# Local attention scored once in 32x32 blocks, a front stage in two bank pairs, and work moved between ScalarE, GpSimd and VectorE

## The reference

```
x = x + attn_a(layernorm(x))   # 16 heads of 8, RoPE, causal over all 256 rows
x = x + ffn(layernorm(x))
x = x + attn_b(layernorm(x))   # 16 heads of 8, causal in windows of 32 rows, q and k rms-normalised with ln_w
x = x + ffn(layernorm(x))
ffn(x): gate, y = q4(x) @ q4(w_gate).T, q4(x) @ q4(w_up).T;  q4(silu(gate) * y) @ q4(w_down).T
```

## Time and profile before

| | us |
|---|---|
| median of three runs | 544.67 |
| the runs | 544.23, 544.67, 548.21 |
| span of the profiled execution, first to last instruction | 543.8 |

### The profile page before, as it was taken

How to read it: one execution, slowest core, us unless ns; L and a number is a source line. 1 busy time by engine, 2 the same in 40 slices (tenths; PEclk the granted TensorE clock), 3 DMA queues, 4 the chain that set the end, 5 groups by cost and what they waited for, 6 DMA issues and landing times.

```text
span 543.8 us, 10363 instructions
## 1 busy us (share of the span) xinstructions
PE 396.0 (73%) x4061; PEld 254.1 (47%) x4061; DVE 356.7 (66%) x894; ACT 202.9 (37%) x548; POOL 176.3 (32%) x207
## 2 busy tenths in 40 slices
PE   0031777587686789979978989889996958769543
PEld 0021434455455446745755665565563544344312
DVE  2982704746754855977899988898779584542531
ACT  1001052171371067266347437536633613414100
POOL 9512031213333053153247333612542514210302
PEclk9999968888897889979989999998997997867755
DMA  7105050030163036026216313410400502400000
GB/s 226 36 0 118 1 120 2 23 97 2 31 149 59 3 99 138 3 61 143 36 34 149 70 31 93 107 21 7 117 13 17 111 2 65 64 14 0 5 6 10
DMA packets 59936, 31.03 MB, mean 57 GB/s; under 512 B 3248, under 2 KB 59504, under 8 KB 59888
## 3 DMA queue, kind: packets, MB, share of 16 engines
q1 hardware_dynamic: 59888, 30.37, 24.1%
HBM read 16.14 MB, written 13.63 MB: 55 GB/s over the span
## 4 chain that ended last, share of the span: by engine, by line
PE 52%; DVE 22%; ACT 8%; DMA 6%; POOL 5%; issue 3%; SPq 3%; POOLq 0%; ACTq 0%; DVEq 0%
PE bank L889 7%; DVE bmax L1252 6%; PE bank L726 4%; PE bank L904 4%; PE bank L850 4%; PE bank L858 4%; PE bank L845 3%; PE bank L694 3%; PE bank L765 3%; PE bank L780 3%; PE bank L897 2%; DMA Qf<-nmTf 2%; PE bank L705 2%; PE bank L807 2%; PE bank L748 2%
## 5 line engine op out<-in xcount | busy, mean ns | idle before, releaser
L1252 DVE TENSOR_REDUCE bmax<-bank 128x3 f32<-128x384 f32 x128 | 62.3, 550 | 13.8 <-PE bank L750 12.7
L963 ACT ACTIVATE prob<-bank 128x384 f32<-128x384 f32 x128 | 56.6, 494 | 23.0 <-PE bank L769 21.6
L1006 ACT ACTIVATE probl<-bank 128x512 f32<-128x512 f32 x64 | 38.2, 598 | 40.3 <-PE bank L850 39.6
L765 PE MATMUL bank<-Qf,Kf 128*128 128x256 bf16 x128 | 28.3, 308 | 24.0 <-DMA Qf<-nmTf 17.5
L1324 DVE SCALAR_TENSOR_TENSOR fb__hg<-fb__th,bank 128x352 f32<-128x352 f32 x16 | 8.3, 520 | 36.2 <-ACT fb__th L1024 35.9
L889 PE MATMUL bank<-wguT,fb__xqT 128*128 128x352 f32 x64 | 27.6, 561 | 3.2 <-DVE fb__h L1325 1.7
L780 PE MATMUL bank<-prob,Vf 128*32 128x128 f32 (+1 forms) x512 | 28.6, 342 | 1.8 <-ACT oTf L924 1.8
L845 PE MATMUL bank<-maskb,identb 128*128 128x512 bf16 x64 | 25.7, 401 | 5.6 <-ACT probl L1006 4.0
L924 ACT ACTIVATE xnTf<-bank 128x256 f32<-128x256 f32 x8 | 3.1, 384 | 71.5 <-PE bank L694 71.5
L1103 POOL TENSOR_TENSOR fb__w<-fb__w,fb__c 128x704 f32<-128x704 f32 x8 | 13.4, 1679 | 49.3 <-DVE fb__w L1214 49.3
L765 PEld LDWEIGHTS bank<-Qf,Kf 128*128 128x128 bf16 x128 | 9.2, 102 | 42.4 <-DMA Qf<-nmTf 19.4
(11 more groups left out here) (212 smaller groups left out, 996.2 us busy)
## 6 DMA issues: line engine op xcount, KB each, us to landing
scr_f<-partsf SPq DMA_DIRECT2D x16, 192.0 KB, 2.4
Qf<-scr_f SPq DMA_DIRECT2D x16, 192.0 KB
Kf<-scr_f SPq DMA_DIRECT2D x16, 192.0 KB
scr_l<-partsl SPq DMA_DIRECT2D x16, 192.0 KB, 3.3
Ql<-scr_l SPq DMA_DIRECT2D x16, 192.0 KB, 3.5
Kl<-scr_l SPq DMA_DIRECT2D x16, 192.0 KB, 4.8
scr_f<-partsf SPq DMA_DIRECT2D x16, 128.0 KB, 1.9
scr_l<-partsl SPq DMA_DIRECT2D x16, 128.0 KB, 2.6
```

The costliest lines, as they stand in the source:

```text
L765: pe.matmul(ring(2 * g + j)[:, 0:256], Kf[:, g, 0:128], Qf[:, 2 * g + j, 0:256], start=True, stop=True)
L963: act.activation(prob[:, h % 8, :], bank[h % 3][:, 0:384], ACT.Exp).then_inc(f.s_exp, 1)
L1006: act.activation(probl[:, u % 2, :, :].rearrange("p c n -> p (c n)"), bank[4][:, :], ACT.Exp).then_inc(l.s_exp, 1)
L1252: dve.tensor_reduce(bmax[:, h, :], bank[h % 4][:, 0:384].rearrange("p (n k) -> p n k", k=P), AX.X, ALU.max).then_inc(bmax_done, 1)
```

## The change

- The local stage keeps q, k and v in fp32 and on the chip: nothing goes through DRAM. The keys are spread into four masked copies (`Kd`, GpSimd), so that one matmul over 32 partitions scores a window of 32 rows against the keys of four heads: 32 matmuls of 32 rows by 32 by 128 columns over all four row quarters and four column quarters of the array, in two halves with a wait between them (l_half). VectorE takes all maxima in one instruction and PE subtracts them with two fp32 matmuls with the identity (512 columns each). ScalarE takes exp of 2 x 512 columns, with q's rms factor as its scale. VectorE transposes in 32x32 blocks (1024 columns), and 128 matmuls of 32x32 by 9 columns, one per window, head and tile, give the outputs already in row order.
- The front stage's first pass runs in banks 0 and 1 and its second pass (now stage front3) in banks 2 and 3. Stacks and v have three homes (RING). Heads use their own 48, 51 or 64 partitions of the array instead of all 128: no zero rows are kept, a head is scored by two matmuls of 256 and 128 columns and masked by two of 256 and 128. The first pass of a batch may run beside the second pass of the batch before it.
- In both FFNs and for the weights, ScalarE makes the rounding constant (`step_of`: Abs, then Exp) that VectorE made from exponent bits or, for the weights, by compares.
- GpSimd centres the layernorms (`norm`) in place of VectorE; ScalarE puts v in its home.
- Masks and the rows of ones come ready from DRAM; GpSimd no longer fills stacks at the start. Loads of later x are steps in SP's order.
- Dependent VectorE instructions are steps of their own. TIMES and FFN_TURNS are new: FFN b's first turn comes after the third of FFN a rather than the fourth.

```diff
+RING = 3
+
+SLOTS = [0, 1, 2, 3, 4, 5, "o0", 6, 7, 8, 9, "o1", 10, 11, 12, 13, "o2", 14, 15, "o3"]
+VL = HD + 1
...
-        zrows = sb("zrows", [3 * PAIRS, SEQ], BF16)
+        Qfs = [sb(f"Qf{i}", [P, PAIRS, SEQ], BF16) for i in range(RING)]
+        Kfs = [sb(f"Kf{i}", [P, PAIRS, SEQ], BF16) for i in range(RING)]
+        Vfs = [sb(f"Vf{i}", [P, T, H, VW]) for i in range(RING)]
...
+                if b >= RING:
+                    sp.wait_ge(f_st_ps, (b - RING + 1) * H)
+                sp.wait_ge(f_wrote, (b + 1) * 16 * 6)
+                for m, dst in enumerate((Qfs[b % RING], Kfs[b % RING])):
...
+                        sp.dma_start(dst[64 * r:64 * r + NSTACK, :, :], src).then_inc(f_stack[b % RING], 16)
...
-                    if g == 0:
-                        pe.wait_ge(f.s_stack[b % 2], (b // 2 + 1) * 96)
-                        pe.wait_ge(f.s_v, b + 1)
-                        pe.wait_ge(rope_mul, b + 1)
-                        if b > 0:
-                            pe.wait_ge(f.s_done, b)
-                    if g >= 2:
-                        pe.wait_ge(bmax_done, b * H + 2 * g - 2)
-                    for j in range(2):
-                        pe.matmul(ring4(2 * g + j)[:, 0:128], Qf[:, 2 * g + j, 0:128], Kf[:, g, 0:128], start=True, stop=True)
-                    for j in range(2):
-                        pe.matmul(ring4(2 * g + j)[:, 128:384], Qf[:, 2 * g + j, 128:256], Kf[:, g, 0:256], start=False, stop=True, skip_group_check=True)
-                    for j in range(2):
-                        pe.matmul(ends(ring4(2 * g + j)), identb[:, :], mask_qk, start=False, stop=True, skip_group_check=True).then_inc(f.s_sc_ps, 1)
+                    if h == 0:
+                        pe.wait_ge(f_stack[b % RING], (b // RING + 1) * 64)
+                        if b < NBATCH - 1:
+                            pe.wait_ge(rope_mul, 2 * (b + 2))
+                            pe.wait_ge(f.s_v, b + 2)
+                        else:
+                            pe.wait_ge(f_nmT, b)
+                        if b == 0:
+                            pe.wait_ge(k_loaded, 16 * (1 + 2 * RING))
+                    if h >= 2:
+                        pe.wait_ge(bmax_done, b * H + h - 1)
+                    g, r = h // 2, h % 2
+                    S = fb[:, r, :]
+                    k = slice(64 * r, 64 * r + NSTACK)
+                    half_ = slice(64 * r, 64 * r + 64)
+                    pe.matmul(S[:, 0:256], Qf[k, g, 128:256], Kf[k, g, 0:256], start=True, stop=True, skip_group_check=True)
+                    pe.matmul(S[:, 256:384], Qf[k, g, 0:128], Kf[k, g, 0:128], start=False, stop=True, skip_group_check=True)
+                    pe.matmul(two(S[:, 128:384], 0, 128), eye_lo[half_, :], twice(m_qk[half_, :]), start=False, stop=True, skip_group_check=True)
+                    mm = pe.matmul(two(S[:, 128:384], 64, 64), eye_hi[half_, :], twice(m_qk[half_, 0:64]), start=False, stop=True, skip_group_check=True)
+                    mm.then_inc(f.s_sc_ps, 1)
                 yield
...
+            def front3(b):
+                Qf, Kf = Qfs[b % RING], Kfs[b % RING]
+                for n, slot in enumerate(SLOTS):
                     yield
...
+                    if n >= 2:
+                        if SLOTS[n - 2] in range(H):
+                            pe.wait_ge(f.s_exp, b * H + SLOTS[n - 2] + 1)
+                        else:
+                            pe.wait_ge(f_oT, b * GROUPS + int(SLOTS[n - 2][1]) + 1)
+                    elif b > 0:
+                        pe.wait_ge((f.s_aT, f.s_done)[n], b)
+                    S = fb[:, 2 + n % 2, :]
+                    if slot in range(H):
+                        if slot == 0:
+                            pe.wait_ge(f_nm_loaded, (b + 1) * 32)
+                        g, r = slot // 2, slot % 2
+                        k = slice(64 * r, 64 * r + KROWS)
+                        half_ = slice(64 * r, 64 * r + 64)
+                        pe.matmul(S[:, 128:384], Kf[k, g, 0:128], Qf[k, g, 0:256], start=True, stop=True, skip_group_check=True)
+                        pe.matmul(S[:, 0:128], Kf[k, g, 128:256], Qf[k, g, 128:256], start=False, stop=True, skip_group_check=True)
+                        pe.matmul(two(S[:, 0:256], 0, 128), eye_hi[half_, :], twice(m_kq[half_, :]), start=False, stop=True, skip_group_check=True)
+                        mm = pe.matmul(two(S[:, 0:256], 0, 64), eye_lo[half_, :], twice(m_kq[half_, 64:128]), start=False, stop=True, skip_group_check=True)
+                        mm.then_inc(f_st_ps, 1)
...
                 if b > 0:
-                    pe.wait_ge(l.s_nmT, b)
-                    if b > 1:
-                        pe.wait_ge(l.s_done, b - 1)
-                turn(bank[5], flat(xnl)).then_inc(l.s_xnT_ps, 1)
+                    pe.wait_ge(l.s_done, b)
...
+                for i in range(2):
+                    pe.matmul(lb[:, i, :], identb, mask_loc.unsqueeze(1).to_broadcast([P, 2, T * P]), start=True, stop=True, skip_group_check=True)
+                for gg in range(2):
+                    c0 = gg * T * P
+                    if gg:
+                        mm.then_inc(l_half, 1)
+                        yield
+                        pe.wait_ge(l_half, b + 1)
+                    for t in range(T):
+                        for n in range(NWIN):
+                            k0 = t * P + n * LS
+                            for i in range(2):
+                                g = 2 * gg + i
+                                rows = slice(32 * g, 32 * g + 32)
+                                mm = pe.matmul(lb[n * LS:(n + 1) * LS, i, c0 + t * P:c0 + (t + 1) * P], qkTl[rows, 0, k0:k0 + LS],
+                                               Kd[rows, :, k0:k0 + LS], start=False, stop=True, skip_group_check=True)
                 mm.then_inc(l.s_sc_ps, 1)
...
-                for u in range(2 * GROUPS + 1):
...
-                            pe.wait_ge(l.s_exp, b * 2 * GROUPS + u)
-                        k = slice((u % 2) * P, (u % 2 + 1) * P)
-                        pe.matmul(bank[4][:, :], identb[:, :], mask_blk, start=True, stop=True)
-                        side = u // 4
-                        r = slice(64 * side, 64 * side + KROWS)
-                        for j in range(4):
-                            g = 4 * (u // 2 % 2) + j
-                            mm = pe.matmul(bank[4][:, j * P:(j + 1) * P], Kl[r, g, k], Ql[r, g, k], start=False, stop=True, skip_group_check=True)
-                        mm.then_inc(l.s_st_ps, 1)
...
+                for i in range(2):
+                    mm = pe.matmul(lb[:, i, :], identf, nmaxl[:, 16 * i:16 * i + 16].unsqueeze(2).to_broadcast([P, 16, LS]),
+                                   start=False, stop=True, skip_group_check=True)
+                mm.then_inc(l_mx_ps, 1)
+                yield
+                pe.wait_ge(l_probT, b + 1)
+                for t in range(T):
+                    for c in range(H):
+                        h = 4 * (2 * (c // 4 % 2) + c // 8) + c % 4
+                        for n in range(NWIN):
+                            rows = slice(n * LS, (n + 1) * LS)
+                            mm = pe.matmul(lb[rows, 0, (t * H + h) * VL:(t * H + h + 1) * VL], probT[rows, c // 4, t, c % 4 * LS:(c % 4 + 1) * LS],
+                                           Vl[rows, t, h, :], start=True, stop=True, skip_group_check=True)
+                mm.then_inc(l.s_o_ps, 1)
...
+            def step_of(dst, src, absd, done, n):
+
+                act.activation(dst, src, ACT.Abs).then_inc(absd, 1)
+                act.wait_ge(absd, n)
+                act.activation(dst, dst, ACT.Exp, scale=STEP * LN2, bias=lift[:, 0:1]).then_inc(done, 1)
...
+                act.wait_ge(l_mx_ps, b + 1)
+                s5 = lb[:, :, :].rearrange("p i (g t k) -> p (i g) t k", g=2, t=T)
+                for t in range(T):
+                    ins = act.activation(probl[:, :, t, :], s5[:, :, t, :], ACT.Exp, scale=rql[:, 1, t:t + 1])
...
+            def norm(b, a, src, mv, rs, dst):
...
+                pool.wait_ge(a.s_rstd, 2 * b + 2)
+                for t in range(T):
+                    ins = pool.tensor_scalar(dst[:, t, :], src[:, t, :], mv[:, t, 0:1], rs[:, 1, t:t + 1], ALU.subtract, ALU.mult)
+                ins.then_inc(a.s_xn, 1)
...
+                pool.wait_ge(l_qkT, b + 1)
+                pool.tensor_tensor(Kd[:, :, :], qkTl[:, 1, :].unsqueeze(1).to_broadcast([P, 4, SEQ]),
+                                   hm.unsqueeze(2).to_broadcast([P, 4, SEQ]), ALU.mult).then_inc(l_kd, 1)
...
-            def centre(b, a, src, mv, rs, dst):
-                dve.wait_ge(a.s_rstd, 2 * b + 2)
-                for t in range(T):
-                    ins = dve.tensor_scalar(dst[:, t, :], src[:, t, :], mv[:, t, 0:1], rs[:, 1, t:t + 1], ALU.subtract, ALU.mult)
...
-                link(dve.tensor_scalar(c[:, :].bitcast(I32), u[:, :].bitcast(I32), 0x7F800000, None, ALU.bitwise_and))
```

(54 more changed lines are left out.)

1252 lines of the change are left out of this document (573 added, 679 removed), and 89 rows, old and new, of tables (FFN_TURNS, TIMES).

## The result

The changed kernel takes 474.6 us (median of 4 runs, 473.34 to 482.57) against 545.75 us for the one before beside it: a ratio of 0.868, 95% interval 0.863 to 0.873. The profiled execution has a span of 472.1 us and took 473.86. Executions of one kernel fall into faster ones and some that take about 2% longer at a lower granted clock; medians here are of all of them, ratios of the fast ones alone. The forecast was 462, with a range of 438 to 515.

A forecast was written before the change was run, and what follows sets the result against it. Neither PE nor DVE was taken as full over the whole; waits mattered, with PE 90% and DVE 84% busy in the steady part. Fill 66 + middle 293 + drain 101 = 460 us, plus a little: 462, range 438 to 515.

The forecast's parts named there:

- Fill: Start to the first front's sum: 66 us for 89.9, first scores at 30, first front done 36 us later.
- PE's work per batch: PE over all stages: local -2.6, front heads +0.9, tiling changes +1.1, net -0.6 us a batch, 348 to 343.
- My bounds for the heads: Front's heads on PE, 768 columns a pass for 640: 0 to 1.8 us more a batch, 0.9 taken.
- DVE's relief: VectorE per batch: about 7.5 us less work, busy 73% for 84%.
- The middle: Seven fronts after the first: 258 us of PE work at a rate of 0.88, 293 us.
- Rival 1: Middle: the chain across engines keeps PE's rate at 0.78, 331 us, total 499; chance 0.15.
- The period I said would be near 41: Middle: expected sign that fronts would follow each other at periods near 41 us, for 44.9 before.
- Drain: After the last front: FFN a, local, FFN b of batch 7 one behind the other, 67 + 32 + 2 = 101 us for 148.
- Rival 2: Middle: FFN banks take turns as before, the period stays 44.9, 314 us, total 482; chance 0.15.
- the sign that I had set: Middle: the prediction counts as wrong if, among other signs, the period of the fronts stays at 45.
- Rival 3: Local stage's output matmuls cost 45 ns each, +7.5 us a batch, total 530; chance 0.06.
- Rival 4: Output matmuls: four row quarters writing one bank wait for each other; slower overall from about 52 ns a record; chance 0.05.

The follow-up runs named there:

- Run 7: Kernel after, with VectorE first clearing a tile 24 times, each with a wait, before its first step: 505.34 us, ratio 0.925.
- runs 3 and 4: Kernel after, output matmuls issued twice (533.64 us), and separately the same 256 issued row quarter by row quarter (524.91 us, ratio 0.963).
- run 10: Kernel after, FFN a's last down phase moved ahead of FFN b's up phase of batch 5, engines' steps reordered to match: 504.33 us, ratio 0.918.
- run 12: Kernel after, with all layernorm centrings and both FFNs' rounding constants put back on VectorE together: 514.08 us, ratio 0.939.
- run 1: Kernel after, with all four centrings of a batch back on VectorE, GpSimd keeping only the root: 490.64 us, ratio 0.902.
- run 4: Kernel after, same 256 output matmuls with the window outermost, 64 in a row in one row quarter and column quarter: 524.91 us, ratio 0.963.

## Why the prediction came out right, and where its steps did not

The forecast was 12 us low in the span, and the three terms are off by +5.8, -10.6 and +16.9. That it came so near is partly luck: the middle's term hides two larger errors against each other, and it in turn makes up for most of the drain's.

**Fill, 66 for 71.8.** First projection at 9.5 as forecast; first scores at 31.9 for 30. The chain of 20.8 us through DRAM became 22.4, with a wait for V at its end. The first front then took 39.9 us for the 36 that I carried over: I gave the first pass of batch 1 beside it 16 x 0.28 us of PE, which went into PE's work but not into the fill's 66; that it is the 3.9 us was not tried. Run 7 shows that what the fill takes counts in full.

**PE's work per batch, -0.6 forecast, about -5.3 measured** (42/8), the term that was mis-sized most. With local taken out of both kernels, local lost 35 us or 4.4 a batch where I had -2.6, although the output matmuls hold PE for 5.6 us where I had 4.0 (records at the 9.5 ns of the earlier trace rows, measured 9.6, and on top waits for issue, 18.0 us in all). The front with the FFNs lost 0.8 a batch where I had +2.0. My bounds for the heads, 0 to 1.8 us more, allowed an overlap only at the last mask of a head. A pair side by side overlaps whole: 0.45 us where the 0.44 ns a column of the earlier trace rows gives 0.68, and less than the 0.56 of before, with the change to the next matmul in it, for which I had added 0.09 us apart. 55 of 128 pairs stand so. That this is what makes -0.8 of +2.0 fits, and no run tried it alone.

**DVE's relief, -7.5 a batch.** The page gives 356.7 - 271.6 = 85 us. Constants, casts and weights at the start take some 33 us of it before and 7 after, which leaves 59, or 7.3 a batch; the size was right. DVE is 185.87/282.4 = 66% busy in the middle, 73% forecast.

**The middle, 293 for 282, by two errors that cancel.** Work 218 for 258, rate 0.77 for 0.88. Rival 1 had the rate right: the rate did not rise when DVE was relieved. It had the reason half right too, as a chain across engines does set the middle: 23.6 and 33.1 us more on DVE cost 16.1 and 25.5 us (0.7 to 0.8 of each), and 58 and 52 us more on PE (runs 3 and 4) cost 50 each, with PE at 87% and DVE at 66%. So neither engine is the bound by itself. That the written order makes the two take turns, so that work on either lies in the period, is my reading of it; no run freed the order. My sum treated PE's work as what the rate divides, and DVE's relief as something that lifts the rate.

The period I said would be near 41, and the mean is 282.4/7 = 40.3. But the mean hides that the steady period did not shrink. The second and third front end 22.4 and 27.6 us after the one before them, where they took 37.7 and 46.4 before: 34 us gained, more than the middle's 24. The five fronts behind took 232.4 us (121.83 to 354.20) for 222.1 before (174.02 to 396.12), 46.5 us each for 44.4. DVE's timelines of the two kernels, first before, then after, where the second and the third front end:

```profile
127.24 0.42 DVE L1265 TENSOR_TENSOR xall<-bank,xall 128x256 f32<-128x256 f32 x1 [1.72 <-PE bank L792]
...
173.60 0.42 DVE L1265 TENSOR_TENSOR xall<-bank,xall 128x256 f32<-128x256 f32 x1
```
```profile
93.82 0.42 DVE L1277 TENSOR_TENSOR xall<-fb,xall 128x256 f32<-128x256 f32 x1
...
121.41 0.42 DVE L1277 TENSOR_TENSOR xall<-fb,xall 128x256 f32<-128x256 f32 x1
```

More passes in those five periods: five locals and nine FFNs end in them, for four and seven and a half before. What the steady part gains shows in the drain, which has that much less left. What lets the second and third front follow so closely was not tried.

**Drain, 101 for 117.9, the step that failed.** Local(7) took 31.4 us for 32, FFN b(7) 33.5 for 33.5, and FFN a(7) 50.7 for 33.5. (The 31.3 us that I called local's second half of before is the distance of two locals' ends in the earlier trace rows; from the first small score at 478.77 to the sum it is 30.2. The sum did not use it.) I had costed a(7) alone, as b(7) is, but behind the last front it shares the engines and the FFN banks with a(6), with the phases of b(4) and b(5) and with local(5) and local(6), in the order of the turns. Its up phase begins 15.8 us after the sum ahead of it, b(7)'s 8.7 (445.09): a(6)'s down phase and local(5)'s outputs stand before it. From there to the first transpose of its down phase a(7) takes 23.4 us (369.99 to 393.43), b(7) 18.3 (445.09 to 463.37), and from there to its sum 11.5 and 6.4. So 7.1, 5.2 and 5.0 make the 17 us. PE's timeline, with b(5)'s up phase ahead of a(7)'s transposes and local(6)'s 256 outputs between its two down parts:

```profile
369.99 0.63 PE L714 MATMUL ffb<-identhm,fa__xq 128*128 128x128 f32 x2
...
390.16 1.45 PE L915 MATMUL ffb<-wguT,fb__xqT 128*128 128x352 f32 x4
...
393.43 0.49 PE L923 MATMUL ffb<-identhm,fa__u 128*128 128x128 f32 x3
395.38 0.94 PE L930 MATMUL ffb<-wdT,fa__hqT 128*128 128x128 f32 x6 [1.45 <-ACT fa__hqT L943]
396.15 0.49 PE L923 MATMUL ffb<-identhm,fa__u 128*128 128x128 f32 x3
397.85 2.40 PE L887 MATMUL lb<-Vl,probT 32*32 32x9 f32 x200 [1.21 <-DVE probT L1302]
402.07 0.93 PE L887 MATMUL lb<-Vl,probT 32*32 32x9 f32 x56 [1.83 <-issue]
402.93 1.65 PE L930 MATMUL ffb<-wdT,fa__hqT 128*128 128x128 f32 x6
...
445.09 0.66 PE L714 MATMUL ffb<-identhm,fb__xq 128*128 128x128 f32 x2 [0.47 <-DVE xall L1349]
...
463.37 0.90 PE L923 MATMUL ffb<-identhm,fb__u 128*128 128x128 f32 x3 [10.06 <-POOL fb__u L1159]
```

That this queue is the 17 us is read from the trace; run 10 tried one other order, which was worse and left a(7) as long, so what a better one would give stays open. The drain's work, 51, was forecast at 50.

**Where the 72 us are from.** The fill 18 (its size read, its worth shown by run 7). Centring and rounding away from VectorE 39.5 (run 12), some 7 of it in the fill by run 1, so not a sum with the first. What is left, some 20 us, is by subtraction and lies with the separate bank pairs of the two passes, the new heads, the new local stage and the new orders together; none of these was tried alone. The shares are prices in the kernel after and need not be those that another order of adding the changes would show. The third home of Q and K gives nothing that shows.

**Rivals.** Rival 2 (period stays 44.9, the FFN banks take turns as before) missed the total, 482, but the last five fronts end 46.5 us apart, near what it said; that the FFN banks are the reason was not tried. By the sign that I had set, a period that stays at 45, the argument on the steady part was wrong, and the first two periods made up for it. PE was 86% and DVE 65% busy between 100 and 350 us, where I had said over 88 and near 75. Rival 3 (45 ns a record) is what the other order of the same records costs, 50 us. Rival 4 did not come and is settled by run 4.

## What to carry to other kernels

Where engines work in one written order and hand tiles to each other within a few microseconds, an engine at two thirds of its time can still be on the path. In this kernel work put on VectorE or PE cost 0.7 to 1 of its duration, whatever the busy share said, and work in a kernel with gaps (the old local stage: 101 us of PE for 27 us of time) little. A mean period over a whole middle can hide that the steady part has not changed; read the periods one by one. A stage that stands alone at the end is costed alone only if nothing is queued in its turn order; read who holds the shared banks when it starts. For hundreds of tiny matmuls, take the row quarters in turn, and count them by how fast instructions arrive, not by their shape.

## What the runs showed of the hardware that was not expected

- Matmuls of 32 rows and 9 columns, four row quarters (each with its own column quarter) in turn into one bank: 9.6 ns a record for the first 200, then some 2 us of waiting for issue; 22 ns on average over 256, 25 over 512. In one row and column quarter one after another: 45 ns.
- Two heads whose stacks lie in the two row halves, with a bank each: 0.45 us for both, 0.43 for one.
- Centring 128 columns takes 0.80 us on GpSimd and between 0.34 and 0.60 on VectorE, by the four places of run 1; having it on GpSimd still gives 16 us.
- Work that nobody needs raised PE's granted clock in the sparse last stretch from 0.50 to between 0.79 and 0.89; it gave 3.1 us in the last FFN and took 1.5 in the local stage before it.
